# A Mamba-style scan layer with attention and a feed-forward net: start-up order, plan places and evacuation order of the scan phase are changed

## The reference

```
xz = x @ W_in + b_in;  u = silu(xz[:1024]);  z = silu(xz[1024:])
B, C = split(u @ W_xproj + b_xproj)          # 16 states each
dt = softplus(u @ W_dt + b_dt)
h[t] = exp(dt[t] * A) * h[t-1] + dt[t] * u[t] * B[t]      # per channel (1024) and state (16)
y[t] = sum over states of h[t] * C[t] + D * u[t]
x = layernorm(x + (y * z) @ W_out + b_out)
x = layernorm(x + cross_attention(x, ctx of 77 tokens, 16 heads))
x = layernorm(x + W2(relu(quantum(W1 x + b1))) + b2)
```

## Time and profile before

| what | value |
|---|---|
| median of three executions | 3189.76 us |
| profiled execution | 3192.79 us |
| its span | 3191.1 us |
| granted TensorE clock, mean | 0.958 of full speed |
| first scan starts | 85.46 us |
| last gate of the scan phase starts | 1995.32 us |
| first work of the next phase | 1998.65 us |
| busy PE, DVE, ACT, POOL | 2836.6, 2687.3, 2016.4, 1836.3 us |

### The profile page before, as it was taken

How to read it: one execution, slowest core, us unless ns; L and a number is a source line. 1 busy time by engine, 2 the same in 40 slices (tenths; PEclk the granted TensorE clock), 3 DMA queues, 4 the chain that set the end, 5 groups by cost and what they waited for, 6 DMA issues and landing times. The chain is left out here.

```text
span 3191.1 us, 48817 instructions
## 1 busy us (share of the span) xinstructions
PE 2836.6 (89%) x18964; PEld 1271.5 (40%) x18964; DVE 2687.3 (84%) x3064; ACT 2016.4 (63%) x3618; POOL 1836.3 (58%) x949
## 2 busy tenths in 40 slices
PE   5888988978988988988978889889999999999998
PEld 2222222222222222222222222556666676667765
DVE  3899999999999999999999988666666677777775
ACT  4676776776766766676676745555555555555564
POOL 3698987887887987988988898221111211112100
PEclk8999999999999999999999989899999999999999
DMA  4111111111111111112112143701111000001000
...
DMA packets 120118, 172.77 MB, mean 54 GB/s; under 512 B 13265, under 2 KB 48721, under 8 KB 119378
## 3 DMA queue, kind: packets, MB, share of 16 engines
...
## 5 line engine op out<-in xcount | busy, mean ns | idle before, releaser
L790 POOL TENSOR_TENSOR h<-h,c_rep 128x1024 f32<-128x1024 f32 x511 | 1197.2, 2357 | 274.6 <-ACT carry L572 273.8
L719 DVE TENSOR_TENSOR_SCAN h<-r_ps,carry,h 128x512 f32<-128x512 f32 x768 | 938.9, 1262 | 8.8 <-ACT r_ps L566 8.5
L566 ACT ACTIVATE r_ps<-r_ps,decay 128x512 f32<-128x512 f32 x1024 | 632.0, 656 | 357.0 <-PE r_ps L340 356.7
L706 DVE TENSOR_TENSOR h<-u_ps,b_rep 128x1024 f32<-128x1024 f32 x512 | 614.4, 1200 | 64.8 <-PE u_ps L351 63.1
L351 PE MATMUL u_ps<-dtu,spread 32*128 32x512 f16 x2048 | 320.5, 391 | 104.2 <-DVE h L706 103.6
L340 PE MATMUL r_ps<-dt,spread 32*128 32x512 f16 x2048 | 314.7, 387 | 57.4 <-DVE h L719 44.7
L367 PE MATMUL y_ps<-h,gather 128*32 128x512 f32 x2048 | 287.0, 628 | 57.4 <-POOL h L790 54.5
L1824 POOL TENSOR_TENSOR o_in<-o_in,rows 128x1024 f32<-128x1024 f32 x15 | 35.9, 2395 | 510.2 <-DMA o_in<-o_dram 510.2
L719 DVE TENSOR_TENSOR_SCAN h<-r_ps,zero,h 128x512 f32<-128x512 f32 x256 | 313.1, 1264 | 7.9 <-ACT r_ps L566 7.8
L40 PE MATMUL fps<-x,region 128*128 128x256 f16 x1024 | 284.1, 277 | 3.5 <-issue 2.4
L41 PE MATMUL fps<-x,region 128*128 128x256 f16 x1024 | 283.5, 277 | 0.0
...
## 6 DMA issues: line engine op xcount, KB each, us to landing
...
z_t_dram<-zs SPq DMA_DIRECT2D x32, 512.0 KB, 3.0
...
result<-x SPq DMA_DIRECT2D x16, 512.0 KB, 2.8
x_t<-dram_x_t SPq DMA_DIRECT2D x15, 512.0 KB, 4.0
```

Source lines behind the costliest of these rows:

```text
L566: nc.scalar.activation(bank, bank, ACT.Exp, scale=decay[:, col:col + 1]).then_inc(s_da, 1)
L706: nc.vector.tensor_tensor(h[:, g % H_GROUPS, o:o + 2, :], u_ps[:, :, :], b_rep[:, c % 2:c % 2 + 1, :].broadcast_to([P, 2, TS]), ALU.mult). ...
L719: nc.vector.tensor_tensor_scan(row, r_ps[:, 2 * (pair % 2) + o, :], row, start, ALU.mult, ALU.add)\
L790: nc.gpsimd.tensor_tensor(rows, rows, c_rep[:, c % 2:c % 2 + 1, :].broadcast_to([P, 2, TS]), ALU.mult)\
```

## The change

- **ScalarE's order in a pair**: `before_exps` and `evacuate_out` come first, then `save_carry`, then `exps`.
- **Start-up**: the first W_in piece is split ahead of x's second half, piece 4 is split before 3, and piece 5 after the first exponentials (its low half on VectorE behind `scans(0)`). dt0 and bc are made in halves of the contraction, the first halves as soon as u0 to u3 are split, in banks of `r_ps`; B and C are spread into `r_ps` too. dt0's sum, product and low halves are VectorE's. Of dt1 only the first half is made ahead; the second is in place 0 of chunk 0.
- **Plans**: plan 0 has new places for z and dt2 to dt7. Plan 1's places are two later. x is read at 21 and 24 (plans 1 and 2) or 19 and 23, instead of 19 and 24. The high half of dt comes three pairs after dt's last place instead of two, but for dt0 and dt1 (`high_at`). The first third of bc waits for the low half of u0 to u3 only.
- **Reloads**: `load_uz` is divided into `load_u` and `load_z` with semaphores of their own; ScalarE's `skip` waits for u alone, the gate for z. SP's order in the first four tiles is written out (`first_steps`).
- **Last chunk**: OUT_AT is 32; the low halves of W_out are in places 20, 21, 23, 25, 27, 29, 30, 31; y tiles are loaded in places 24, 26, ...; the loads of W_k and W_v are in places 59 and 62. b_out is added to the first two tiles by a matmul with one row (64 in the weights), and VectorE adds them to x straight from PSUM (`x0_tile`); GpSimd's two additions go.

The diff, cut to what the prediction speaks of:

```diff
-W_OUT_AT, OUT_AT = 18, 28
-X0_AT = 38
+W_OUT_AT, OUT_AT = 18, 32
+W_OUT_LOW_AT = (20, 21, 23, 25, 27, 29, 30, 31)
...
-            self.z = ((0,), (1,), (5,), (6,), (10,), (11,), (12, 13), (14, 15))
+            self.z = ((1, 2), (3, 4), (8, 9), (13,), (14,), (15,), (19,), (20,))
-            self.dt = ((-9,), (-9,), (2, 3, 4), (7, 8, 9), (16, 17, 18), (19, 20, 21), (22, 23, 24), (25, 26, 27))
+            self.dt = ((-9,), (0,), (5, 6, 7), (10, 11, 12), (16, 17, 18), (21, 22, 23), (24, 25, 26), (27, 28, 29))
...
-            self.x, self.u_high = (19, 24), (36, 44)
+            d = 2 if n == 1 else 0
+            self.x, self.u_high = (21, 24) if n <= 2 else (19, 23), (36 + d, 44 + d)
+            self.u = tuple((28 + d + 2 * t, 29 + d + 2 * t) for t in range(8))
...
+    def high_at(self, t):
+        return self.dt[t][-1] + (2 if t < 2 else 3)
...
                 if s in plan.bc:
-                    pe.wait_ge(s_ul, 2 * n + 2)
+                    pe.wait_ge(s_ul, 2 * n + 1 + min(plan.bc.index(s), 1))
...
+                    if i < 2:
+                        if i == 0:
+                            pe.wait_ge(s_first, 32)
+                            pe.wait_ge(s_fb, 1)
+                        last = nc.tensor.matmul(pj[:, :], x_t[0:1, 1, 0:P], x_t[0:1, 0, :], start=False, stop=True)
...
-            pe.wait_ge(s_wl, 3)
-            project(first, "bc", w_xp, 0, u16, 0, NJ, NJ, y_ps[0:2 * NSTATE, :], 2 * NSTATE)
-            pe.wait_ge(s_wl, 4)
-            for t in range(2):
...
+            pe.wait_ge(s_ul, 1)
+            pe.wait_ge(s_wl, 4)
+            project(first, "dt0", w_dt, 0, u16, 0, half, NJ, dt0_ps, free=1)
+            project(first, "bc", w_xp, 0, u16, 0, half, NJ, bc_ps, 2 * NSTATE, free=2)
+            pe.wait_ge(s_ul, 2)
+            project(first, "dt0", w_dt, 0, u16, half, NJ, NJ, dt0_ps)
+            project(first, "bc", w_xp, 0, u16, half, NJ, NJ, bc_ps, 2 * NSTATE)
+            project(first, "dt1", w_dt, P, u16, 0, half, NJ, pj[:, :], free=NJ)
...
+            evacuate_dt(first, 0, r_ps[:, 0, :])
+            softplus(first, 0)
+            evacuate_bc(first, r_ps[0:2 * NSTATE, 1, :])
+            dt_high(first, 0)
...
             exps(0)
             exps(1)
+            weights_high(5)
             for pair in range(TOTAL):
-                save_carry(pair)
                 for plan, s in producing(pair):
                     before_exps(plan, s)
                 s = pair - (NC - 1) * PAIRS
-                if OUT_AT <= s < OUT_AT + 2 * OUT_TILES and (s - OUT_AT) % 2:
+                if OUT_AT + 4 <= s < OUT_AT + 2 * OUT_TILES and (s - OUT_AT) % 2:
                     evacuate_out((s - OUT_AT) // 2)
+                save_carry(pair)
...
+            def x0_tile(i):
+                dve.wait_ge(s_op, i + 1)
+                if i == 0:
+                    dve.wait_ge(s_first, 32)
+                nc.vector.scalar_tensor_tensor(a["x0"][:, i, :], pj[:, :], UNSCALE, a["x0"][:, i, :], ALU.mult, ALU.add)\
+                    .then_inc(s_oe, 1)
...
                 scans(pair)
+                if pair == 0:
+                    weights_low(pieces[5][2], pieces[5][0], pieces[5][3], 6)
+                s = pair - (NC - 1) * PAIRS
+                if s == OUT_AT + 1:
+                    x0_tile(0)
+                if s == OUT_AT + 3:
+                    x0_tile(1)
```

201 lines of the change are left out of this document (112 added, 89 removed).

## The result

The changed kernel takes 3165.25 us, median of four executions (3163.83 to 3169.00), against 3188.98 (3187.53 to 3192.28) for the kernel before on the same chip: ratio 0.9926, 95% interval 0.9909 to 0.9943. It is faster by 24 us. The forecast was 3126 with a range of 3106 to 3150, so the time lies 15 us above the range. The profiled execution has a span of 3162.1 us against 3191.1, 29.0 less; the terms of the forecast are compared with these 29.0. They are 5 us more than the medians differ by: the trace of the kernel before is of an execution of 3192.79 us, longer than all four that the median is from.

What follows compares the result with a forecast made beforehand. VectorE bounds the kernel with its 512 pairs, so only its idle time can be won. Terms: -26.5 + 2.3 - 7 - 30 - 5 + 2.4 = -63.8 from 3192.8, giving a median of 3126 us; range 3106 to 3150.

Steps and rivals of the forecast that it cites:

- Start-up: Stretch before VectorE's first scan: scan starts near 58.9 instead of 85.46 us, -26.5; the moved W_in split gives back +2.3.
- Chunk 0: First scan chunk: VectorE stalls 8.2 us against 15.6, -7; the last W_in split behind the first scans adds +2.3.
- rival 3: Chunk 0 gives back: three neighbouring z places and the store wait cost 15 more, 3141 us; 12%.
- Steady chunks: Chunks 1 to 6: VectorE's idle gaps go except one of 1.24 us a chunk, -30, bounds -34 and -12.
- Rival 2: Steady gaps only move, GpSimd's lag being the same work in other places: -12 instead of -30, 3144 us; 13%.
- gap (a): Chunk 1 at 438.01: ScalarE waits 2.13 us for GpSimd's dt7 product; later copy gives 3.6 us or more of room.
- gap (c): Chunk 1 at 531.49: VectorE idle 1.24 us where nine matmuls run at the slow level; nothing acts on it.
- (b): Chunk 1 at 512.14: TensorE waits 3.35 us for u's low half; split B/C gives 3.6 us, just enough, the thinner margin.
- Evacuation ahead of the carry copy: ScalarE's order in a pair: GpSimd's product is delayed within some 5 us of room; costed at zero in chunks 0 to 6.
- Last chunk: Output stage: VectorE idle 25.6 to some 20.5, -5; tail +2.4, as ScalarE evacuates the last piece before the last carry copy.
- Rival 4: Last chunk: x0 and b_out come late and TensorE stands at the first output tile: +14, 3140 us; 12%.
- The markers: Signs to check, among them first scan near 59 us; disproof: a steady chunk still at 237 us or first scan after 66.

Runs made afterwards that it cites:

- e8: Changed kernel with chunk 0's z tile 3 at place 10 instead of 13 and dt tile 3 one place later: 3154.74 us, ratio 0.989.
- e12: Changed kernel with GpSimd's low half of x's second part made for 8 of 512 columns from chunk 1 on: 3140.57 us, ratio 0.9846.
- e10: Changed kernel with x places, dt half copies, u wait and carry copy order taken back in the steady part: 3169.4 us, ratio 0.9933.
- e4: Kernel before with only the high and low half copies of dt tiles 2 to 7 one place later: 3209.91 us, ratio 1.0068.
- e3: Kernel before with only the split wait of B/C for the halves of u: 3177.0 us, ratio 0.9958.
- e2: Kernel before with only ScalarE's new order, evacuation ahead of the carry copy: 3199.05 us, ratio 1.0035.
- e7: Changed kernel with nine more matmuls at each of places 51 and 52, their sums overwritten: 3166.64 us, ratio 0.9922.
- e1: Changed kernel with ScalarE's carry copy ahead of the evacuations again: 3168.25 us, ratio 0.9932.
- e9: Changed kernel with transfers of b_out and x's first two tiles issued ahead of the weight pieces in the last chunk: 3161.4 us, ratio 0.9914.
- e13: Changed kernel with z tile 3 at place 10 in chunk 0 and b_out and x transfers first in the last chunk: 3151.48 us, ratio 0.9875.
- e15: e13 with GpSimd's eight low halves of w_out made for 8 of 512 columns only: 3143.68 us, ratio 0.9854.
- e18: e13 with the split u wait as the only steady edit; x places, dt half copies and carry copy order taken back: 3138.96 us, ratio 0.9837.

## Why the prediction was wrong, step by step

**Start-up (-26.5): right**, by the mechanism given: TensorE at its fast level, dt0 ahead of B/C, halves of the contraction. That it came to the tenth is luck: this execution began its matmuls 1.5 to 2 us later than the later ones, and the last steps were shorter than forecast (4.8 us from the low halves to the scan, not 5.5). By the later traces the term is about -28. Of the 0.7 us for splitting W_in first, 0.3 to 0.8 show at their first matmul. The last W_in split cost its 2.3 behind the first pair.

**Chunk 0 (-7 and +2.3): wrong in size and sign.** The mechanism was named, z4's evacuation behind the store of z2 and z3, and priced at 4 us. It cost 9.3 in three waits (e8: 11 us by the stretch, with the two smaller waits behind them). The price left out what a stall of TensorE brings after itself: 4.1 us idle, then matmuls at the slow level, 3.95 and 2.07 us of waits. x's second half was priced at 1.5, and 4.7 us of waits stand at places 28 to 34; with x's low half cut (e12) 2.3 of them are left, so GpSimd has a share there too. Together with the gaps that chunk 1 kept this was rival 3 in kind, and nearly in size: 11.5 us above the forecast in the stretch.

**Steady chunks (-25 of the -30 in the measured stretch): the main error.** Measured -5.7, and e10, without the edits, takes only 3.2 more than the changed kernel there. Rival 2, "GpSimd's lag is the same work in other places", was the right mechanism, and it got 13% and a price of -12 for six chunks, both too kind to the forecast. The failed step is: "3.6 us or more of room for a wait of 2.1". It looked at ScalarE, whose wait for one product is indeed gone, and took this wait to be all of gap (a). But GpSimd has no free time from place 20 to 31. Over the places 17 to 29 it has thirteen multiplications at 2.31 by starts, three sums and products of dt at 2.6, three pairs of subtractions at 2.3 and two x halves at 2.1, 49 us, and thirteen pairs of VectorE take 45 (3.48 by starts where it never waits; the prediction's 3.6 was too long, its own durations less three overlaps of 0.07 give 3.5). Moving a subtraction inside them moves their end by nothing, and the sums wait for the third of three multiplications running (882.09). The experiments say so in both directions: moving work later costs 23 us (e4), taking 2.1 us a chunk of it away gives 25 (e12). And the four edits were added as if each had its own gap; alone, in the kernel before, they are worth -10 to -13 (e3), +11 (e2) and +23 (e4), while together they gained 2 to 6. x's place was not tried alone, and how much of the difference it carries, and how much lies in how the edits act on each other, is not shown.

What was said of gap (c), "nothing acts on it", failed too. TensorE's granted clock now fell in the light places 51 and 52, at the very sums that VectorE waits for: +1.2 a chunk in five chunks, shown by e7. That the missing stop at (b) brought this about is likely from e3, but not the only way to it: in e2 gap (c) rose to 2.1 with (b) standing. That (b) itself would go, the thinner one, was right.

**Evacuation ahead of the carry copy (0): right for this kernel** (e1), wrong as a general statement: in the kernel before the same edit costs 11 us (e2). It was priced by the room that GpSimd's product has; why the waits at (b) and (c) grow in e2 was not looked into.

**Last chunk (-5 and +2.4): +4.5.** The wait before the first output tile was foreseen ("some 8 us and then some 2", measured 9.04 and 2.15), and so was its cause, but the stall did not shrink: the waits at the start of the output were 2.75 + 7.02 + 1.71 = 11.5 us before and are 4.28 + 9.04 + 2.15 = 15.5 now, since the 4.28 ahead of the first tile was left out of the sum. The credit for GpSimd's two additions did come: waits of 1.70 and 3.33 us that stood there before (at 1910.35 and 1928.81) are one of 1.47 now, 3.6 us less, as forecast. Rival 4's cause was real and small: the transfer costs 1.5 us (e9). Of the three waits of e13, 13.9 us, GpSimd's low halves of W_out make 6 (e15); what makes the rest is open. The tail: the chain behind the last scan waits 2.75 for the carry copy, +2.5 where 2.4 was forecast, and 0.9 less for the sums, so the last gate came 1.6 later after it, not 2 to 3; but one pair earlier VectorE now waits 2.2 for exponentials, which the text had not, and which the kernel before does not show. It stands in e1 and e18 as well, with the carry copy in front again, so the order does not make it.

**The markers.** First scan near 59, ScalarE's and TensorE's named waits gone, 8 us before the first addition: seen. "Idle of chunk 0 between 5 and 15" failed, 17.5 us. "VectorE idle there about 1.3 us a chunk" was the main one that failed, 4.5 to 7.0. The text named a steady chunk of 237 us as what would prove it wrong. That was no test: from B to B the kernel before itself takes 232.7 once and 235.3 to 235.5 four times, and the changed one takes 232.5 to 235.0. e12, with part of GpSimd's work left out, has 229.3 in four of five and 1147.9 in all, where the forecast's steady chunks come to 1174.4 - 25 = 1149.4.
